# Softmax denominators of the two token halves in different rows: reciprocal over 256 columns, and the spread steps in new places

## The chip, the core and the metric

The kernel runs on one core of a Trainium2 chip. The core has a matrix engine (TensorE, PE in the profile; its weight loads are PEld), a vector engine (VectorE, DVE), an engine for activations (ScalarE, ACT), a general one (GpSimd, POOL) and SyncE (SP), which here only issues transfers. Each works through its own queue in order; they meet at semaphores. The metric is device microseconds (us) of one execution, as the median of several runs.

## The reference

The inputs are x (8 batches of 512 tokens of 512 values) and a context (8 batches of 120 tokens). Cut to what matters:

```python
Q = (layernorm(x) @ Wq.T + bq)   # 16 heads of 32
K, V = ctx @ Wk.T + bk, ctx @ Wv.T + bv
scores = einsum('bhqd,bhkd->bhqk', Q, K) / sqrt(32)
out = einsum('bhqk,bhkd->bhqd', softmax(scores), V)
expert = mean over 8 experts of (out @ We.T + be)
x = x + tanh(g_xattn) * (expert @ Wo.T + bo)
# then a gated feed-forward: logits = layernorm(x) @ w_gate, the best of 8 experts by
# argmax, at most 100 tokens per expert, layernorm(x) rows @ w_expert, scaled by the gate
x = x + tanh(g_ffn) * ffn(layernorm(x))
```

## The kernel before

A prologue of some 110 us transposes weights, builds keys and values of all batches and the product of the experts' mean with Wo (`mixT`). Then a loop runs over the 8 batches, software-pipelined: in the turn of batch 0 (step argument `b`) the queries of batch 1 are made, and so on. The order of the steps on each engine is a table written out by hand, of entries (step, how many batches ahead, part): `(spread_rden, 0, 2)` is part 2 of the spread for the current batch, `(q_tile, 1, 2)` the query tile 2 of the next batch. Each engine has its own table for the turns 0 to 6 (the loop), and another for the last turn (batch 7), where the rows that were chosen for an expert are gathered and multiplied too. Nothing but these tables and the semaphore waits in the steps sets the order. Nearly all products are written by one helper, so that they all have its line (L756); the names of their tiles tell them apart.

Steps that the change and the prediction speak of, with g or t for one of four parts:

- `scores` (ps<-q_stack,k_stack) makes the scores of four heads; `exp` on ACT writes them as `probs` (120 context tokens x 4 heads x 512 tokens, f32).
- `weight_sums` (ps<-probs,den_sel) sums probs over the context tokens, with one 120x32 matrix of a constant and zeros as weights. It adds up in `den_b` over the four g. The four matmuls (j = 0 to 3) write four different groups of 32 rows, and so run side by side. The profile has two records for each f32 matmul. Row 32j+m of `den_b` holds the sum of head 4g+j with g = m % 4: eight copies of each, over 512 tokens.
- `value_sums` (ps<-probs,v_all) makes the unnormalised attention, copied to `attn` by `value_out` (ACT).
- `reciprocal` (DVE) takes 1/x of the whole of `den_b`, 128x512. `rden_high` (ACT, f16) and `rden_low` (DVE) write from it `rden_both`, in which some copies hold the f16 value and others the rest.
- `spread_rden` (ps<-rden_both,head_sel) picks one head's two rows for each of the 128 output rows and writes them to a bank of 512 columns, once for each g. Parts 0 and 1 wait for `rden_low`; parts 2 and 3 for the `divide` that reads the bank before.
- `divide` (DVE, attn<-ps,attn) multiplies. `attn_high` (ACT) and `attn_low` (POOL, in the last turn DVE) cast the result to an f16 pair.
- `mix_high`, `mix_low` (ps<-mixT_..,attn_hi and ps<-mixT_hi,attn_lo) are the 8 and 4 products that make output tile t; part k of either waits for `attn_high` or `attn_low` of g = k. Each of the four tiles needs all four g.
- `q_tile` (12 products, ps<-xnT_..,wqT_..) is `q_begin` (6) and `q_end` (6). `q_high` (ACT) and `q_low` (DVE) read it out. `max_scores` (ps<-k_hi,q_hi, 16 small matmuls) makes rough scores, from which `maxima` (DVE, neg_max) takes a maximum; `max_scores` g waits for `maxima` g-1. `max_turn` (ps<-ident,neg_max) waits for the last one. After it `shift_row` (ACT) and a transfer write the row `shift` into `q_stack`, for which the next batch's `scores` waits. Ten more transfers (`q_stack<-q_hi`, `q_stack<-q_lo`) are issued by SP once `q_high` 3 and `q_low` 3 are done, ahead of that of `shift`.
- In the last turn `row_norm` (ACT, xb<-rows) normalises gathered rows, `row_turn` (ps<-ident,xb) turns them and `row_product` (ps<-wqT_..,xnT_..) multiplies them.

Of the kernel before, what the change touches and what calls it, by code (L numbers as in the profile page):

```python
# [79 lines left out]
def build(nc, x, ctx, g_xattn, g_ffn, Wq, bq, Wk, bk, Wv, bv, We, be, Wo, bo, w_gate, w_expert, b_expert, out):  # L80
# [7 lines left out]
    with ExitStack() as st:  # L88
        def sb(name, shape, dt):
            return st.enter_context(nc.sbuf_tensor(name, shape, dt))  # L90
# [663 lines left out]
        def _(e):  # L754
            def mm(out_, a, b, start=True, stop=True, **kw):
                return e.matmul(out_, a, b, start=start, stop=stop, **kw)  # L756
# [236 lines left out]
            def late_unit(i):  # L993
# [12 lines left out]

                (q_tile, 1, 1), (q_tile, 1, 2), (max_scores, 1, 1),
                (spread_rden, 0, 0), (spread_rden, 0, 1), (q_begin, 1, 3), (spread_rden, 0, 2), (spread_rden, 0, 3),
                (q_end, 1, 3),

                (mix_high, 0, 0), (mix_low_begin, 0, 0), (max_scores, 1, 2), (mix_low_end, 0, 0), (mix_high, 0, 1),
                (max_scores, 1, 3), (route_attn, 0, 0), (mix_low, 0, 1), (mix_begin, 0, 2), (max_turn, 1, 0),
# [35 lines left out]
            def last_product(_, t):  # L1048
# [10 lines left out]
                (value_sums, 0, 3),  # L1059
                (row_turn, 0, 0), (spread_rden, 0, 0), (spread_rden, 0, 1), (row_turn, 0, 1), (row_product, 0, 0),  # L1060
                (spread_rden, 0, 2), (spread_rden, 0, 3), (row_turn, 0, 2), (row_product, 0, 1), (row_turn, 0, 3),
                (mix_high, 0, 0), (mix_low, 0, 0), (mix_high, 0, 1), (mix_low, 0, 1), (route_attn, 0, 0),
# [8 lines left out]
        def _(e):  # L1071
# [137 lines left out]
            def x2_high(b, t):  # L1209
# [23 lines left out]
                (exp, 0, 1), (value_out, 0, 0), (gate_exp, -1, 0), (exp, 0, 2), (value_out, 0, 1),  # L1233
                (exp, 0, 3), (value_out, 0, 2), (value_out, 0, 3),
                (rden_high, 0, 0), (row_norm, 0, 0), (row_high, 0, 0), (row_norm, 0, 1), (attn_high, 0, 0),
                (attn_high, 0, 1), (row_high, 0, 1), (row_norm, 0, 2), (attn_high, 0, 2), (attn_high, 0, 3),
# [7 lines left out]
        def _(e):  # L1244
            e.memset(wgc[:, :, :], 0.0).then_inc(s_setv, 1)
            e.memset(den_sel[:, :, :], 0.0).then_inc(s_setv, 1)
            e.wait_ge(s_setv, 2)
            for g in range(NK):
                e.memset(den_sel[:, g, g::NK], 1.0 / (ATTN_SCALE * RDEN_SCALE)).then_inc(s_setv, 1)
            e.wait_ge(s_set, 2)  # L1250
            for g in range(NK):
                e.tensor_tensor(head_sel[:, g, :].rearrange("p (j d) -> p j d", d=DK),
                                ident[:, g::DK].unsqueeze(2).to_broadcast([P, HJ, DK]),
                                ident[:, NK + g::DK].unsqueeze(2).to_broadcast([P, HJ, DK]),
                                ALU.add).then_inc(s_setv, 1)
# [6 lines left out]
            e.wait_ge(s_setv, 13)  # L1262
            for half, unit_of in enumerate((1.0 / GATE_SCALE, 1.0 / (ATTN_SCALE * MIX_SCALE))):
# [227 lines left out]
            def add_table(b, _):  # L1491
# [97 lines left out]
            def last_out(b, t):  # L1589
# [192 lines left out]
```

## Time and profile before

| what | value |
|---|---|
| median of 3 runs | 443.79 us (441.75 to 445.31) |
| the profiled execution | 441.84 us, of it 440.1 us span |
| mean granted TensorE clock | 0.992 of full speed |
| PE busy | 420.4 us (96%) |
| DVE busy | 342.0 us (78%) |
| ACT busy | 223.3 us (51%) |
| POOL busy | 162.0 us (37%) |

The span is from the first to the last instruction of the program; the execution's own time is 1.74 us more. The durations below are those of the profiled execution. Busy time of PE counts each matmul from its start to the modelled end of its result, about 0.17 us after the next one may start, so the pace of the engine is read from one start to the next. In the loop the same step starts 38.1 us apart from one turn to the next (`max_scores` 3 at 208.22, 246.35, 284.49 us). In the last turn the first product of the mix starts at 398.27 us, and from there PE works to its last product without a gap between two starts that is longer than the work.

### The profile page before, as it was taken

The page shows a single profiled execution, that of the slowest core. Times are in us where ns is not written, and L with a number is a line of the kernel's source. Part 1 is how long each engine was busy: PE and PEld are TensorE (multiplying, and loading weights), DVE is VectorE, ACT ScalarE, POOL GpSimd, SP SyncE. Part 2 cuts the span into 40 slices and gives each one's busy share as a digit, 9 for nine tenths or more (in the row PEclk, how much of TensorE's full clock was granted, in tenths as well). Part 3 has the DMA queues.
Part 4 walks back from the last instruction along what each step waited for, and adds up shares of the span by engine and source line. Part 5 has one row for each costly group of instructions (what it writes and reads, how often), then busy time and mean ns, then how long its engine had stood idle before and what let it go on. Part 6 is the DMA issues. An engine that isn't in the chain of part 4 may idle for free.

```text
span 440.1 us, 8128 instructions
## 1 busy us (share of the span) xinstructions
PE 420.4 (96%) x2839; PEld 192.0 (44%) x2839; DVE 342.0 (78%) x675; ACT 223.3 (51%) x279; POOL 162.0 (37%) x149
## 2 busy tenths in 40 slices
PE   5899999899999999999999999999999998879996
PEld 4567464342344334434534443453444344334442
DVE  6438345785697999889889988988994698759983
ACT  4335313566572945666384475637537383556200
POOL 1005899315062319307132630703351082260460
PEclk9999999999999999999999999999999999969999
DMA  8998991356019605923860682295078044042573
GB/s 234 329 387 308 300 392 41 72 102 174 1 37 184 224 2 124 223 97 67 158 220 0 140 215 89 58 206 180 1 153 193 1 97 142 9 142 44 102 179 114
DMA packets 64843, 63.15 MB, mean 143 GB/s; under 512 B 41218, under 2 KB 44430, under 8 KB 64804
## 3 DMA queue, kind: packets, MB, share of 16 engines
q1 hardware_dynamic: 59691, 56.19, 48.0%
q0 software_dynamic: 1632, 3.49, 2.8%
q10 hardware_dynamic: 3480, 2.96, 2.1%
q8 instruction: 24, 0.39, 0.4%
q14 instruction: 16, 0.12, 0.1%
HBM read 29.59 MB, written 12.98 MB: 97 GB/s over the span
## 4 chain that ended last, share of the span: by engine, by line
PE 84%; ACT 5%; DVE 4%; DMA 3%; issue 2%; SPq 1%; ACTq 0%; POOLq 0%; DVEq 0%
PE ps L756 65%; PE ps L416 9%; DVE neg_max L1396 4%; ACT probs L1073 4%; PE ps L514 3%; PE ps L378 2%; DMA ctx_raw<-in_ctx_dram 1%; PE ps L961 1%; DMA rows<-out_dram,row_ix 1%; PE ps L537 1%; PE ps L488 1%; DMA q_stack<-shift 1%; PE ps L1019 1%; SPq L645 1%; ACT xb L1073 0%
## 5 line engine op out<-in xcount | busy, mean ns | idle before, releaser
L1073 ACT ACTIVATE probs<-ps 120x2048 f32<-120x2048 f32 x32 | 60.1, 1878 | 42.8 <-PE ps L756 42.8
L1705 POOL TENSOR_TENSOR attn_lo<-attn,attn_hi 128x512 f16<-128x512 f32 x28 | 31.5, 1158 | 112.6 <-ACT attn_hi L1073 112.6
L1396 DVE TENSOR_REDUCE neg_max<-ps 128x16 f32<-128x1920 f32 x32 | 68.6, 2142 | 1.0
L756 PE MATMUL ps<-xnT_hi,wqT_hi 128*128 128x512 f16 x128 | 48.6, 380 | 0.1
L756 PE MATMUL ps<-mixT_hi,attn_hi 128*128 128x512 f16 x128 | 48.5, 379 | 0.0
L756 PE MATMUL ps<-mixT_lo,attn_hi 128*128 128x512 f16 x128 | 48.5, 379 | 0.0
L756 PE MATMUL ps<-xnT_lo,wqT_hi 128*128 128x512 f16 x128 | 48.5, 379 | 0.0
L1650 POOL TENSOR_SCALAR veps<-mv 128x4 f32<-128x4 f32 (+1 forms) x17 | 4.6, 268 | 117.1 <-DVE mv L1283 81.4
L1713 POOL TENSOR_TENSOR xb<-xb,mix_bias 128x512 f32<-128x512 f32 x32 | 39.5, 1267 | 17.3 <-DVE cb_col L1339 17.3
L1073 ACT ACTIVATE q_hi<-ps,bias_cols 128x512 f16<-128x512 f32 x32 | 21.9, 686 | 36.0 <-PE ps L756 35.9
L756 PE MATMUL ps<-q_stack,k_stack 97*120 97x512 f16 x128 | 33.9, 387 | 2.2 <-DMA q_stack<-shift 0.8
L756 PE MATMUL ps<-mixT_hi,attn_lo 128*128 128x512 f16 x128 | 34.1, 380 | 0.3
L756 PE MATMUL ps<-probs,den_sel 120*32 120x512 f32 x256 | 34.1, 605 | 0.1
L756 PE MATMUL ps<-probs,v_all 120*32 120x512 f32 x256 | 33.3, 592 | 0.7 <-ACT attn L1073 0.7
L756 PE MATMUL ps<-xnT_hi,wqT_lo 128*128 128x512 f16 x128 | 32.8, 379 | 0.0
L1390 DVE SCALAR_TENSOR_TENSOR q_lo<-ps,bias_cols,q_hi 128x512 f16<-128x512 f32 x32 | 23.9, 746 | 11.4 <-ACT q_hi L1073 11.4
L1346 DVE RECIPROCAL rden<-ps 128x512 f32<-128x512 f32 x8 | 26.9, 3358 | 7.4 <-PE ps L756 7.4
L1073 ACT ACTIVATE q_stack<-q_hi 32x2048 f16<-32x2048 f16 x16 | 30.5, 1907 | 0.5
L1362 DVE SCALAR_TENSOR_TENSOR xb<-ps,xb 128x512 f32<-128x512 f32 x32 | 22.0, 686 | 8.6 <-PE ps L756 8.6
L1073 ACT ACTIVATE attn<-ps 128x512 f32<-128x512 f32 x32 | 19.0, 595 | 18.3 <-PE ps L756 18.2
L1073 ACT ACTIVATE attn_hi<-attn 128x512 f16<-128x512 f32 x32 | 19.7, 630 | 13.0 <-DVE attn L1356 13.0
L756 PEld LDWEIGHTS ps<-q_stack,k_stack 97*120 97x120 f16 x128 | 14.9, 132 | 20.0 <-ACT probs L1073 10.9
(246 smaller groups left out, 808.3 us busy)
## 6 DMA issues: line engine op xcount, KB each, us to landing
xb<-in_x_dram SPq DMA_DIRECT2D x8, 1024.0 KB, 6.0
q_stack<-q_hi SPq DMA_DIRECT2D x48, 128.0 KB
out_dram<-xb SPq DMA_DIRECT2D x6, 1024.0 KB, 5.9
raw<-in_L_xattn_We_dram SPq DMA_DIRECT2D x5, 1024.0 KB, 11.7
q_stack<-q_lo SPq DMA_DIRECT2D x32, 128.0 KB
xb<-in_L_xattn_We_dram SPq DMA_DIRECT2D x3, 1024.0 KB, 9.4
k_stack<-k_scratch SPq DMA_DIRECT2D x8, 360.0 KB, 4.0
out_dram<-xb SPq DMA_DIRECT2D x8, 256.0 KB, 2.2
```

What stands on the lines that cost most here:

```text
L378: ins = e.transpose(b[0:rows, i * cols:(i + 1) * cols], src_of(i), ident[0:cols, 0:cols])
L416: ins = e.matmul(out_, a(pa, k), b(pb_, k), start=(i == 0), stop=(i == len(steps) - 1))
L514: ins = e.matmul(b[:, :], left(i, o), right[j][:, o, :], start=(n == 0), stop=(n == len(steps) - 1))
L756: return e.matmul(out_, a, b, start=start, stop=stop, **kw)
L1073: return e.activation(out_, in_, func, **kw)
L1346: e.reciprocal(rden[:, :], den_b).then_inc(s_rec, 1)
L1362: e.scalar_tensor_tensor(out=row, in0=pair_b[t % 2], scalar=1.0 / (ATTN_SCALE * MIX_SCALE), in1=row, op0=ALU.mult, op1=ALU.add).then_inc(s ...
L1390: e.scalar_tensor_tensor(out=q_lo[:, g, :], in0=pair_b[g % 2], scalar=bias_cols[:, g:g + 1], in1=q_hi[:, g, :], op0=ALU.add, op1=ALU.subtr ...
L1396: e.tensor_reduce(neg_max[:, :, :, g], quad[:, :, 0:NT * SK].rearrange("p j (t s) -> p t j s", t=NT), AX.X, ALU.max, negate=True).then_inc ...
L1650: e.tensor_scalar(tmp, mean_var, EPS, None, ALU.add).then_inc(s_ve, 1)
L1705: e.tensor_tensor(attn_lo[:, g, :], attn[:, g, :], attn_hi[:, g, :], ALU.subtract).then_inc(s_alo, 1)
L1713: ins = e.tensor_tensor(row, row, mix_bias[:, :], ALU.add)
```

## The change

The denominators of tokens 0 to 255 go to rows 32j+m with m < 16, those of tokens 256 to 511 to rows with m >= 16, both in columns 0 to 255 of `den_b`. For this `weight_sums` issues for each g eight matmuls of 256 columns (h = 0, then h = 1, each with another selection matrix) in place of four of 512. The reciprocal and the two casts of it go over 256 columns, and `spread_rden` writes its bank by two matmuls of 256 columns, with a `head_sel` for each half. The tables change too: in the loop, spread parts 0 and 1 now stand inside query tile 2 and ahead of `max_scores` 1, `max_scores` 2 stands ahead of `mix_high` 0 (not inside `mix_low` 0), `maxima` 1 on DVE stands ahead of `q_low` 2 and the divides 2 and 3, and `rden_high` on ACT ahead of `q_high` 1; in the last turn the spreads stand ahead of `row_turn` 0 and 1.

```diff
-        den_sel = sb("den_sel", [SK, NK, DK], F32)
-        head_sel = sb("head_sel", [P, NK, P], F16)
+        den_sel = sb("den_sel", [SK, 2 * NK * DK + 24], F32)
+        head_sel = sb("head_sel", [P, 2, NK, P], F16)
...
-                for j in range(HJ):
-                    row = slice(j * DK, (j + 1) * DK)
-                    ins = mm(den_b[row, :], den_sel[:, g, :], probs[:, g % 2, j, :], start=(g == 0), stop=(g == NK - 1))
+                for h in range(2):
+                    sel = den_sel[:, (h * NK + g) * DK:(h * NK + g + 1) * DK]
+                    for j in range(HJ):
+                        row = slice(j * DK, (j + 1) * DK)
+                        ins = mm(den_b[row, 0:SH], sel, probs[:, g % 2, j, h * SH:(h + 1) * SH],
+                                 start=(g == 0 and h == 0), stop=(g == NK - 1 and h == 1))
...
-                mm(bank, head_sel[:, g, :], rden_both[:, :]).then_inc(s_bc, 1)
+                mm(bank[:, 0:SH], head_sel[:, 0, g, :], rden_both[:, :])
+                mm(bank[:, SH:S], head_sel[:, 1, g, :], rden_both[:, :]).then_inc(s_bc, 1)
...
-                e.reciprocal(rden[:, :], den_b).then_inc(s_rec, 1)
+                e.reciprocal(rden[:, :], den_b[:, 0:SH]).then_inc(s_rec, 1)
...
-                (reciprocal, 0, 0), (maxima, 1, 0), (rden_low, 0, 0), (q_low, 1, 1),
-                (divide, 0, 0), (divide, 0, 1), (q_low, 1, 2), (divide, 0, 2), (divide, 0, 3), (maxima, 1, 1),
+                (divide, 0, 0), (divide, 0, 1), (maxima, 1, 1), (q_low, 1, 2), (divide, 0, 2), (divide, 0, 3),
```

On PE in the loop, before: query tile 2 (its last products are the first row), `max_scores` 1, spreads 0 and 1, the first half of query tile 3, spreads 2 and 3.

```order
L756 MATMUL ps<-xnT_hi,wqT_lo 128x512 x4
L756 MATMUL ps<-k_hi,q_hi 128x120 x16
L756 MATMUL ps<-rden_both,head_sel 128x512 x2
L756 MATMUL ps<-xnT_hi,wqT_hi 128x512
L756 MATMUL ps<-xnT_lo,wqT_hi 128x512
L756 MATMUL ps<-xnT_hi,wqT_hi 128x512
L756 MATMUL ps<-xnT_lo,wqT_hi 128x512
L756 MATMUL ps<-xnT_hi,wqT_hi 128x512
L756 MATMUL ps<-xnT_lo,wqT_hi 128x512
L756 MATMUL ps<-rden_both,head_sel 128x512 x2
```

The same place of PE with the change, from the spreads 0 and 1 on:

```order
L757 MATMUL ps<-rden_both,head_sel 128x256 x4
L757 MATMUL ps<-xnT_hi,wqT_hi 128x512
L757 MATMUL ps<-xnT_lo,wqT_hi 128x512
L757 MATMUL ps<-xnT_hi,wqT_lo 128x512 x4
L757 MATMUL ps<-k_hi,q_hi 128x120 x16
```

The spreads moved up past half a query tile, and `max_scores` 1 moved down behind them.

On DVE in the loop, before, from the reciprocal to `maxima` 2 (neg_max is `maxima`, attn is `divide`):

```order
L1346 RECIPROCAL rden<-ps 128x512
L1396 TENSOR_REDUCE neg_max<-ps 128x16
L1351 SCALAR_TENSOR_TENSOR rden_both<-rden,low_row,rden_hi 128x512
L1390 SCALAR_TENSOR_TENSOR q_lo<-ps,bias_cols,q_hi 128x512
L1356 TENSOR_TENSOR attn<-ps,attn 128x512 x2
L1390 SCALAR_TENSOR_TENSOR q_lo<-ps,bias_cols,q_hi 128x512
L1356 TENSOR_TENSOR attn<-ps,attn 128x512 x2
L1396 TENSOR_REDUCE neg_max<-ps 128x16
L1390 SCALAR_TENSOR_TENSOR q_lo<-ps,bias_cols,q_hi 128x512
L1396 TENSOR_REDUCE neg_max<-ps 128x16
```

And with the change:

```order
L1346 RECIPROCAL rden<-ps 128x256
L1396 TENSOR_REDUCE neg_max<-ps 128x16
L1351 SCALAR_TENSOR_TENSOR rden_both<-rden,low_row,rden_hi 128x256
L1390 SCALAR_TENSOR_TENSOR q_lo<-ps,bias_cols,q_hi 128x512
L1356 TENSOR_TENSOR attn<-ps,attn 128x512 x2
L1396 TENSOR_REDUCE neg_max<-ps 128x16
L1390 SCALAR_TENSOR_TENSOR q_lo<-ps,bias_cols,q_hi 128x512
L1356 TENSOR_TENSOR attn<-ps,attn 128x512 x2
L1390 SCALAR_TENSOR_TENSOR q_lo<-ps,bias_cols,q_hi 128x512
L1396 TENSOR_REDUCE neg_max<-ps 128x16
```

`maxima` 1 (the second neg_max) moved from behind the divides 2 and 3 to ahead of them.

On PE in the last turn, with the change, from the last `value_sums` to the first `row_product` (xb is `row_turn`); before, the order was row_turn 0, spreads 0 and 1, row_turn 1, row_product 0, spreads 2 and 3, row_turn 2:

```order
L757 MATMUL ps<-probs,v_all 32x512 x8
L757 MATMUL ps<-rden_both,head_sel 128x256 x4
L1016 MATMUL ps<-ident,xb 128x100 x4
L757 MATMUL ps<-rden_both,head_sel 128x256 x4
L1016 MATMUL ps<-ident,xb 128x100 x4
L757 MATMUL ps<-wqT_hi,xnT_hi 128x512
```

Both pairs of spreads now stand ahead of the first row product.

## Rows read from the trace of the kernel before

**Rows 1.** The page: busy time of PE and the others.

```profile
PE 420.4 (96%) x2839; PEld 192.0 (44%) x2839; DVE 342.0 (78%) x675; ACT 223.3 (51%) x279; POOL 162.0 (37%) x149
```

**Rows 2.** Timeline of PE in one turn: start, us, what, idle before and its releaser.

```profile
230.15 1.06 PE L756 MATMUL ps<-probs,den_sel 120*32 120x512 f32 x8
231.03 1.04 PE L756 MATMUL ps<-probs,v_all 120*32 120x512 f32 x8
232.01 0.39 PE L756 MATMUL ps<-xnT_hi,wqT_hi 128*128 128x512 f16 x1
...
237.29 0.39 PE L756 MATMUL ps<-k_hi,q_hi 32*128 32x120 f16 x16
237.61 0.61 PE L756 MATMUL ps<-rden_both,head_sel 128*128 128x512 f16 x2
...
243.60 0.39 PE L756 MATMUL ps<-k_hi,q_hi 32*128 32x120 f16 x16
244.04 0.39 PE L756 MATMUL ps<-mixT_hi,attn_lo 128*128 128x512 f16 x1
...
246.35 0.39 PE L756 MATMUL ps<-k_hi,q_hi 32*128 32x120 f16 x16 [0.20 <-DVE neg_max L1396]
```

**Rows 3.** Timeline of DVE in the same turn.

```profile
231.28 3.36 DVE L1346 RECIPROCAL rden<-ps 128x512 f32<-128x512 f32 x1 [0.86 <-PE ps L756]
...
239.91 1.28 DVE L1356 TENSOR_TENSOR attn<-ps,attn 128x512 f32<-128x512 f32 x2
241.10 2.15 DVE L1396 TENSOR_REDUCE neg_max<-ps 128x16 f32<-128x1920 f32 x1
243.17 0.74 DVE L1390 SCALAR_TENSOR_TENSOR q_lo<-ps,bias_cols,q_hi 128x512 f16<-128x512 f32 x1
244.05 2.16 DVE L1396 TENSOR_REDUCE neg_max<-ps 128x16 f32<-128x1920 f32 x1
```

**Rows 4.** Timelines of ACT, POOL and SP in the same turn.

```profile
240.62 1.23 ACT L1073 ACTIVATE attn_hi<-attn 128x512 f16<-128x512 f32 x2 [0.63 <-DVE attn L1356]
241.75 0.67 ACT L1073 ACTIVATE q_hi<-ps,bias_cols 128x512 f16<-128x512 f32 x1
...
239.47 4.51 POOL L1705 TENSOR_TENSOR attn_lo<-attn,attn_hi 128x512 f16<-128x512 f32 x4 [15.07 <-ACT attn_hi L1073]
...
246.25 3.49 SPq L645 DMA_DIRECT2D q_stack<-q_lo  x4
250.26 0.52 SPq L645 DMA_DIRECT2D q_stack<-shift  x1
```

**Rows 5.** Groups by line and form, whole span: count, busy us and mean ns of one, idle before.

```profile
L1451 DVE RECIPROCAL gate<-l_sum 128x4 f32<-128x4 f32 x8 | 1.4, 180 | 0.3
L756 PEld LDWEIGHTS ps<-probs,den_sel 120*32 120x32 f32 x256 | 5.0, 108 | 10.5 <-issue 9.6 <-ACT probs L1073 0.3
```

**Rows 6.** Timelines of ACT and PE in the last turn.

```profile
384.72 0.60 ACT L1073 ACTIVATE attn<-ps 128x512 f32<-128x512 f32 x1 [1.19 <-PE ps L756]
386.29 0.81 ACT L1073 ACTIVATE xb<-rows,row_shift,table 100x512 f32<-100x512 f32 x1
...
387.15 0.93 PE L1019 MATMUL ps<-ident,xb 100*128 100x100 f32 x4 [2.50 <-ACT xb L1073]
387.88 1.06 PE L756 MATMUL ps<-rden_both,head_sel 128*128 128x512 f16 x2
389.37 0.93 PE L1019 MATMUL ps<-ident,xb 100*128 100x100 f32 x4 [0.44 <-ACT xb L1073]
390.10 0.63 PE L756 MATMUL ps<-wqT_hi,xnT_hi 128*128 128x512 f16 x1
...
394.36 0.59 PE L756 MATMUL ps<-rden_both,head_sel 128*128 128x512 f16 x2
394.79 0.51 PE L1019 MATMUL ps<-ident,xb 100*128 100x100 f32 x4
```

**Rows 7.** One stretch of the last turn: busy time by engine, granted clock, DMA.

```profile
388.00:390.00 2.00, 1.56 (x7) 0.65 (x6) 1.35 (x3) 1.35 (x3) 1.46 (x2) 0.50 0.46 150
```

More of the change, by code:

```diff
@@ L59 @@
 HALF = B // 2
+SH = S // 2
 QK_SCALE = 16.0
@@ L1005, in _ @@
                 (places, -1, 0), (q_end, 1, 0), (values, 0, 2), (max_scores, 1, 0), (values, 0, 3),
[L1007 to L1011, printed above, removed]
+                (q_tile, 1, 1), (q_begin, 1, 2), (spread_rden, 0, 0), (spread_rden, 0, 1), (q_end, 1, 2),
+                (max_scores, 1, 1), (q_begin, 1, 3), (spread_rden, 0, 2), (spread_rden, 0, 3), (q_end, 1, 3),
+                (max_scores, 1, 2), (mix_high, 0, 0), (mix_low, 0, 0), (mix_high, 0, 1),
                 (max_scores, 1, 3), (route_attn, 0, 0), (mix_low, 0, 1), (mix_begin, 0, 2), (max_turn, 1, 0),
@@ L1059, in _ @@
                 (value_sums, 0, 3),
-                (row_turn, 0, 0), (spread_rden, 0, 0), (spread_rden, 0, 1), (row_turn, 0, 1), (row_product, 0, 0),
-                (spread_rden, 0, 2), (spread_rden, 0, 3), (row_turn, 0, 2), (row_product, 0, 1), (row_turn, 0, 3),
+                (spread_rden, 0, 0), (spread_rden, 0, 1), (row_turn, 0, 0), (spread_rden, 0, 2), (spread_rden, 0, 3),
+                (row_turn, 0, 1), (row_product, 0, 0), (row_turn, 0, 2), (row_product, 0, 1), (row_turn, 0, 3),
                 (mix_high, 0, 0), (mix_low, 0, 0), (mix_high, 0, 1), (mix_low, 0, 1), (route_attn, 0, 0),
@@ L1225, in _ @@
                 (value_out, 0, 2), (value_out, 0, 3), (gate_exp, -1, 0),
-                (q_high, 1, 1), (rden_high, 0, 0), (q_high, 1, 2), (attn_high, 0, 0), (attn_high, 0, 1),
+                (rden_high, 0, 0), (q_high, 1, 1), (attn_high, 0, 0), (q_high, 1, 2), (attn_high, 0, 1),
                 (attn_high, 0, 2), (attn_high, 0, 3), (q_high, 1, 3),
@@ L1233, in _ @@
                 (exp, 0, 1), (value_out, 0, 0), (gate_exp, -1, 0), (exp, 0, 2), (value_out, 0, 1),
-                (exp, 0, 3), (value_out, 0, 2), (value_out, 0, 3),
-                (rden_high, 0, 0), (row_norm, 0, 0), (row_high, 0, 0), (row_norm, 0, 1), (attn_high, 0, 0),
+                (exp, 0, 3), (value_out, 0, 2), (rden_high, 0, 0), (value_out, 0, 3),
+                (row_norm, 0, 0), (row_high, 0, 0), (row_norm, 0, 1), (attn_high, 0, 0),
                 (attn_high, 0, 1), (row_high, 0, 1), (row_norm, 0, 2), (attn_high, 0, 2), (attn_high, 0, 3),
@@ L1245, in _ @@
             e.memset(wgc[:, :, :], 0.0).then_inc(s_setv, 1)
-            e.memset(den_sel[:, :, :], 0.0).then_inc(s_setv, 1)
+            e.memset(den_sel[:, :], 0.0).then_inc(s_setv, 1)
             e.wait_ge(s_setv, 2)
-            for g in range(NK):
-                e.memset(den_sel[:, g, g::NK], 1.0 / (ATTN_SCALE * RDEN_SCALE)).then_inc(s_setv, 1)
+            for h in range(2):
+                first = h * (NK * DK + DK // 2)
+                e.memset(den_sel[:, first:first + NK * (DK + 1)].rearrange("p (g c) -> p g c", g=NK)[:, :, 0:DK // 2:NK],
+                         1.0 / (ATTN_SCALE * RDEN_SCALE)).then_inc(s_setv, 1)
             e.wait_ge(s_set, 2)
[L1251 to L1254, printed above, removed]
+            for h in range(2):
+                row_of = ident[:, :].rearrange("p (j h c g) -> p h c g j", h=2, c=NK, g=NK)
+                e.tensor_tensor(head_sel[:, h, :, :].rearrange("p g (j d) -> p g j d", d=DK),
+                                row_of[:, h, 0, :, :].unsqueeze(3).to_broadcast([P, NK, HJ, DK]),
+                                row_of[:, h, 1, :, :].unsqueeze(3).to_broadcast([P, NK, HJ, DK]),
                                 ALU.add).then_inc(s_setv, 1)
@@ L1600, in _ @@
                 (read_places, -1, 0), (enter_places, -1, 0), (expert_low, 0, 1), (add_table, -1, 0), (row_index, 0, 0),
-                (reciprocal, 0, 0), (rden_low, 0, 0), (row_lo, 0, 0), (divide, 0, 0), (divide, 0, 1), (row_lo, 0, 1),
-                (last_attn_low, 0, 0), (last_attn_low, 0, 1), (divide, 0, 2), (divide, 0, 3), (last_attn_low, 0, 2),
+                (reciprocal, 0, 0), (rden_low, 0, 0), (divide, 0, 0), (divide, 0, 1), (row_lo, 0, 0), (divide, 0, 2),
+                (divide, 0, 3), (row_lo, 0, 1), (last_attn_low, 0, 0), (last_attn_low, 0, 1), (last_attn_low, 0, 2),
                 (last_attn_low, 0, 3), (row_lo, 0, 2), (row_bias, 0, 0), (row_out, 0, 0), (row_lo, 0, 3),
```

19 lines of the change are left out of this document (7 added, 12 removed).

## Prediction

> **What bounds the kernel now.** I read the page first: PE is busy for 96% of the span, so only work of PE and waits of PE count, and another engine counts through them [rows 1]. Next comes the timeline of PE in one turn of the loop, of which seven follow each other at a period of 38.1 us, alike to some hundredths [rows 2]. The reader is to see how small the holes are. Between 230 and 250 us PE waits four times: about 0.07 us for `q_low` 1 behind the spreads 0 and 1, 0.12 us for the last `attn_low` at 244.04, about 0.27 us for `maxima` 2 at 246.35, and 0.05 us for `maxima` 3, some 0.5 us in all. I take each as the time from one start to the next less that of the same step elsewhere; only the third shows in brackets, since a result takes longer than the pace. Then I read who ends these waits, on DVE, ACT and POOL [rows 3, 4]. Last comes the final turn, where PE has its one long hole: no record starts between the last `value_sums` and 387.15, and behind it the granted clock is 0.50, the lower of the two levels (1.2 against 2.4 GHz) [rows 6, 7]. From 398.3 us PE runs without a hole to its last product, so what is won or lost ahead of that counts in full.
>
> **Work of PE.** In `weight_sums` four f32 matmuls of 512 columns become eight of 256. The columns are the same, and the four groups of 32 rows still run side by side. The four of 512 take 0.88 us from start to start (230.15 to 231.03) [rows 2]; each of their two rounds costs some hundredths beyond the array's own time. Two rounds more per g would cost from 0.004 us (what the second round shows) to 0.03 us (the first). I take the lower, since in the middle of a run the next weights are in place: 32 x 0.004 = 0.13 us in all. The spreads become 4 x 0.108 us instead of 2 x 0.216 (two took 0.43, from 394.36 to 394.79 [rows 6]); 0.1 us in all for twice as many matmuls. The changes of shape of PE's tile stay as many.
>
> A rule speaks against the halving. The four matmuls have the same 120 rows of the array and differ in its columns, and their weights show 108 ns each [rows 5]; yet two rounds of them and their loads pass in 0.88 us, so the loads lie under the matmuls. The Trainium skill, "TensorE: Matmul & The Clock Gate", section "Part 3: Packing small matmuls — row/col tiling", says that a weight load overlaps matmuls in flight only where its row group differs, and by it each new round would lay its load open. By that rule the sum would grow by the second rival's price below; the trace of before disagrees with it.
>
> **DVE, ACT and the spreads.** The reciprocal of 4 columns takes 0.18 us, that of 512 takes 3.36 us [rows 3, 5], so one column costs (3.36 - 0.18) / 508 = 6.3 ns and 256 take 1.76 us: 1.60 us less. It starts at 231.28 as before, ends at 233.0, `maxima` 0 is done at 235.2 (2.15 us) and `rden_low`, with half of its columns, at about 235.6. PE comes to the spreads 0 and 1 after three halves of query tiles: tile 1 starts at 232.01, and two tiles take up to 237.29, so 18 of 24 products end at 235.9 [rows 2]. No wait: the shorter reciprocal pays for the earlier place. With 3.36 us the same spreads would have waited about 1.5 us. `rden_high` ahead of `q_high` 1 waits until 233.0, while query tile 1 ends at 234.8, so it holds nobody up. The wait for `q_low` 1 goes: -0.07 us.
>
> **The chain that now ends last.** `max_scores` 1 starts at 237.29 + 0.43 = 237.72, behind the spreads. The rest is a walk through the new order with the old durations:
> - DVE: `maxima` 1 starts 0.45 us after its `max_scores` (243.60 to 244.05), at 238.17; DVE had nothing to do for 0.5 us before. It holds DVE for 2.07 us (241.10 to 243.17), `q_low` 2 for 0.66 (0.74 less the 0.08 by which such instructions overlap), and the divides 2 and 3 run from 240.90 to 242.18. Before, these ended at 239.91 + 1.28 = 241.19 [rows 3]. The 1.6 us won go into `maxima` 1, and the divides come 1.0 us later.
> - ACT and POOL: `attn_high` 3 ended at 241.85, and now ends at 242.84. POOL ran its four `attn_low` without a pause, 1.13 us each, from 239.47 to 243.98 [rows 4]. Now the first two run early, POOL pauses, and part 2 starts only when `attn_high` 2 is there, at 242.31. Part 3 ends at 242.31 + 4.51 / 2 = 244.6, which is 0.6 us later.
> - PE: behind `max_scores` 1 (0.32) come half of tile 3, two spreads and the other half (2.59 + 0.43), and `max_scores` 2 at 241.16, ended at 241.48. The eight products of `mix_high` 0 end at 243.34, with 0.14 us of waiting for `attn_high` 3. After three products of `mix_low` 0, at 243.99, PE waits for `attn_low` 3 until 244.65. Before, the same product started at 244.04 [rows 2]. That is 0.61 us late.
> - Given back: `mix_high` 1 then ends late enough that `maxima` 2 (244.1 to 246.3) is done before `max_scores` 3 wants it, so the wait of 0.27 us goes. `max_scores` 3 starts at 246.69 and not at 246.35: **0.34 us late**. `maxima` 3, `max_turn` and all that follows stay late by as much.
>
> The transfers to `q_stack` move too. They start when `q_high` 3 ends, before at 242.42 (241.75 + 0.67), now at about 243.4, since `q_high` 3 stands behind `attn_high` 3. The ten of them keep SP busy until 249.74 + 1.0 = 250.75, where `shift` went out at 250.26 and would now be ready at 250.60 [rows 4]. So the transfer of `shift` goes from waiting for ACT to waiting for the queue, 0.5 us late, and `scores` finds it just in time, with its 0.2 us of slack used up. I count nothing and keep 0.3 us a turn for the range.
>
> Loop: 7 x 0.34 = 2.4 us, and 0.2 us for the matmuls, **+2.6 us**.
>
> **The last turn.** The spreads 0 and 1 can start when `value_out` 3 ends at 385.3 (384.72 + 0.60) instead of at 387.88. But `row_turn` 0 waits for ACT's `row_norm` (386.29 to 387.11), which waits for a gathered row, and `row_turn` 1 for the next one; neither knows of the denominators [rows 6]. So the first row product stays at 390.10 if the clock stays as it was, and only the spreads 2 and 3 leave the path behind it (394.36 to 394.79): **-0.43 us**. The clock is the open point. While it is low, `row_turn` 0 and 1 take 0.73 us each, 0.37 more than at full clock, and the 12 products 4.26 us (390.10 to 394.36) against 2.59: together 2.4 us. If it stays high, the first turn ends 0.37 us earlier, ACT's next step follows, the products start at about 389.35, and the mix starts at 395.3: -3.0 us in place of -0.43. The hole from 384.6 to 387.15 now has 0.43 us of spreads in it, and the one from 387.5 to 389 has 0.43 more. That is little; I hold the fall of the clock for somewhat likelier than not.
>
> **Sum.** 441.84 + 2.6 - 0.4 = 444.0 us for an execution like the profiled one. The median of the runs before lies 1.95 us above that execution, and I carry the difference over: 443.79 + 2.15 = **445.9 us**.
>
> **Rivals.**
> - The clock stays high in the last turn. For it: PE has two more bits of work in the hole. Against it: the hole stays mostly empty, since the gathered rows set it. 443.79 + 2.6 - 3.0 = 443.4 us. Chance 0.27.
> - Slower: the weight loads of the added rounds lie open. Place: the 32 groups of `weight_sums`, two more rounds in each. Price: up to 108 ns a round, 64 x 0.108 = 6.9 us, so 452.8 us; from 35 ns a round on it is over 1% slower than before. Against it: the 0.88 us of the rows. This is the result of the page's rule above. Chance 0.06.
> - Slower: `q_stack` becomes the end of the chain. With `shift` landing or the ten transfers 0.3 to 0.6 us later than I have it, PE waits at each `scores` 0: 2 to 4 us more, 448 to 450 us. Chance 0.12.
> - Faster: POOL's last cast is in time after all, because the divides or `maxima` 1 run earlier than in my walk. Then the 0.3 us of waits go and none comes: 7 x -0.3 - 0.4 to -3.0, so 441.3 to 438.7 us. The walk would have to be wrong by 0.6 us. Chance 0.09.
> - The change doesn't do what it says, the time of the reciprocal not going by columns: 7 x 1.5 us, 456 us. The 0.18 us of the small one excludes it nearly: 0.01.
> - The forecast itself, 444.5 to 447.5 us: 0.45.
>
> **How the numbers follow.** No change that a measurement of this kernel can tell is one within 1%, 4.4 us. The forecast, the high clock, most of the faster case and a third of the `q_stack` case lie inside. Faster by over 1% has 0.06, slower 0.15, no change 0.79. The range goes from 441.0 (into the faster case, below the high clock with a shorter wait) to 449.5 us, most of the `q_stack` case; what is left out is the open weight loads and the ends, under 0.2.
>
> **What would show it.** A reciprocal of 1.7 to 1.8 us; eight den_sel matmuls in 0.88 to 0.91 us; no wait at the spreads 0 and 1. A pause of POOL between the second and third `attn_low`, and a wait of PE of 0.5 to 0.8 us for the last one in each turn; none for `maxima` 2. A period of 38.5 us instead of 38.1. In the last turn a spread right behind `value_out` 3, and either a stretch of 6 to 7 us at 0.50 or none. I am wrong if the period is shorter than 38.1, or if PE waits for `q_stack` in the loop.

## The result, and the profile after

| what | before | after |
|---|---|---|
| median of 20 runs of each, on the same chips | 442.88 us (441.22 to 445.31) | 445.18 us (443.50 to 448.99) |
| ratio, 95% interval | | 1.0059 (1.0042 to 1.0076) |
| profiled execution | 441.84 us, span 440.1 | 445.22 us, span 443.5 |
| period of the loop (max_scores 3 to the next) | 38.13 us | 38.5 us; one turn 38.92 |

The kernel became slower by 2.3 us by the medians, by 2.6 us (1.9 to 3.4) by the ratio: 0.6%. That is under the 1% which the prediction took as the least that can be told, but with 20 runs of each the interval of the ratio excludes 1. The forecast was 445.9 us, +2.15. The first line of the page after, against [rows 1]: DVE lost 13.0 us of work (342.0 to 329.0, eight reciprocals at 1.6 us each) and the span grew.

```profile
PE 422.4 (95%) x3127; PEld 204.6 (46%) x3127; DVE 329.0 (74%) x671; ACT 221.4 (50%) x279; POOL 163.3 (37%) x149
```

Groups by line and form after, over the whole span (count, busy us and mean ns of one, idle before), against [rows 5]:

```profile
L1346 DVE RECIPROCAL rden<-ps 128x256 f32<-128x256 f32 x8 | 14.1, 1757 | 7.5 <-PE ps L757 7.5
L757 PEld LDWEIGHTS ps<-probs,den_sel 120*32 120x32 f32 x512 | 13.4, 109 | 16.0 <-issue 9.6 <-ACT probs L1070 0.3
```

The reciprocal is at 1.757 us and the loads have doubled in number. Next PE after, in the turn of [rows 2] (start, us, what, idle before and its releaser). The whole turn starts 1.80 us later here: 231.95 answers to 230.15.

```profile
231.95 1.07 PE L757 MATMUL ps<-probs,den_sel 120*32 120x256 f32 x16
232.84 1.04 PE L757 MATMUL ps<-probs,v_all 120*32 120x512 f32 x8
...
237.49 0.38 PE L757 MATMUL ps<-xnT_lo,wqT_hi 128*128 128x512 f16 x1
237.70 0.60 PE L757 MATMUL ps<-rden_both,head_sel 128*128 128x256 f16 x4
...
245.15 0.81 PE L757 MATMUL ps<-mixT_hi,attn_lo 128*128 128x512 f16 x3
246.45 0.39 PE L757 MATMUL ps<-mixT_hi,attn_lo 128*128 128x512 f16 x1 [0.49 <-POOL attn_lo L1705]
...
248.50 0.39 PE L757 MATMUL ps<-k_hi,q_hi 32*128 32x120 f16 x16
```

Three things stand here. Sixteen records of `weight_sums` go from 231.95 to 232.84, 0.89 us where eight took 0.88. The spreads follow a product of the query tile at the usual 0.21 us: no wait. And the product behind `mix_low` 0's first three comes 1.30 us after their start, where three take 0.65: PE waits 0.65 us for POOL. `max_scores` 3 (248.50) has lost its bracket for neg_max.

DVE after in the same turn, against [rows 3], from the reciprocal through `maxima` 1 and the second pair of divides:

```profile
233.09 1.76 DVE L1346 RECIPROCAL rden<-ps 128x256 f32<-128x256 f32 x1 [0.88 <-PE ps L757]
...
239.97 2.16 DVE L1396 TENSOR_REDUCE neg_max<-ps 128x16 f32<-128x1920 f32 x1 [0.56 <-PE ps L757]
...
242.71 1.28 DVE L1356 TENSOR_TENSOR attn<-ps,attn 128x512 f32<-128x512 f32 x2
```

ACT and POOL after, against [rows 4]:

```profile
243.42 1.23 ACT L1070 ACTIVATE attn_hi<-attn 128x512 f16<-128x512 f32 x2 [2.57 <-DVE attn L1356]
```

```profile
239.55 1.16 POOL L1705 TENSOR_TENSOR attn_lo<-attn,attn_hi 128x512 f16<-128x512 f32 x1 [13.36 <-ACT attn_hi L1070]
240.92 1.15 POOL L1705 TENSOR_TENSOR attn_lo<-attn,attn_hi 128x512 f16<-128x512 f32 x1 [0.21 <-ACT attn_hi L1070]
244.12 2.27 POOL L1705 TENSOR_TENSOR attn_lo<-attn,attn_hi 128x512 f16<-128x512 f32 x2 [2.05 <-ACT attn_hi L1070]
```

Read from below: POOL pauses 2.05 us for `attn_high` 2; ACT waited 2.57 us for the divides; DVE made the divides behind `maxima` 1; and `maxima` 1 waited 0.56 us for its `max_scores`, which PE issues behind the spreads now. The reciprocal gave up 1.60 us ahead of the divides, and 2.07 us of `maxima` 1 took its place.

Then what the forecast counted at nothing. SP and PE after, at the hand-over of queries to `scores` two turns earlier (an SPq line is the time that SP took to issue a transfer, not the time to its landing):

```profile
171.64 3.81 SPq L646 DMA_DIRECT2D q_stack<-q_lo  x4
175.50 0.59 SPq L646 DMA_DIRECT2D q_stack<-shift  x1
```

```profile
178.04 1.04 PE L757 MATMUL ps<-q_stack,k_stack 97*120 97x512 f16 x4 [0.24 <-issue]
...
372.12 1.04 PE L757 MATMUL ps<-q_stack,k_stack 97*120 97x512 f16 x4 [1.36 <-DMA q_stack<-shift]
```

The four `q_lo` transfers are issued from 171.64 to 175.45 without a pause for ACT, `shift` right behind them, where in [rows 4] 0.5 us lie between the two: in this turn the queue, and not ACT, sets when `shift` goes. So it went out late and PE lost 0.42 us (38.92 for 38.5). The bracket says issue, but the product could only start once the row had landed, which the trace puts at 177.70. In the turn of [rows 4] it is not so:

```profile
249.04 2.50 SPq L646 DMA_DIRECT2D q_stack<-q_lo  x4
252.41 0.52 SPq L646 DMA_DIRECT2D q_stack<-shift  x1
```

Here the queue is free at 251.54, `shift` waits for ACT as before, and PE loses nothing. What differs is how long SP takes to issue the ten transfers: 6.24 us here (245.30 to 251.54), 7.57 us two turns earlier.

The last row above is the last turn: its `scores` are 3.83 us behind those of before (372.12 to 368.29), `max_scores` 3 ahead of it 3.30 us (364.05 to 360.75), so 0.53 us more were lost. This is another thing. `shift` goes out 0.06 us after ACT has written it, but takes longer to land, as the chain that ended last shows, before and then after:

```profile
364.66 3.27 DMA q_stack<-shift
```

```profile
367.99 3.78 DMA q_stack<-shift
```

From issue to landing the last `shift` takes 2.9 to 3.8 us in the profiles of the twelve kernels, 3.68 in e4 and 3.54 in e9, which don't have the late queue; in the turns of the loop it is 2.1 to 2.2 us almost everywhere. So these 0.5 us can't be put down to the change.

Last the final turn, PE against [rows 6]:

```profile
389.31 0.60 PE L757 MATMUL ps<-rden_both,head_sel 128*128 128x256 f16 x4 [0.81 <-ACT attn L1070]
391.12 0.93 PE L1016 MATMUL ps<-ident,xb 100*128 100x100 f32 x4 [1.21 <-ACT xb L1070]
391.84 1.06 PE L757 MATMUL ps<-rden_both,head_sel 128*128 128x256 f16 x4
393.34 0.93 PE L1016 MATMUL ps<-ident,xb 100*128 100x100 f32 x4 [0.44 <-ACT xb L1070]
394.06 0.63 PE L757 MATMUL ps<-wqT_hi,xnT_hi 128*128 128x512 f16 x1
...
398.57 0.51 PE L1016 MATMUL ps<-ident,xb 100*128 100x100 f32 x4
```

And a stretch of it, with the granted clock as the number behind POOL's, against [rows 7]:

```profile
392.00:394.00 2.00, 1.56 (x9) 0.96 (x7) 1.38 (x3) 1.92 (x4) 1.70 (x2) 0.50 0.60 154
```

The spreads are where the table puts them, the clock is at its lower level again (0.50), and the row products of turn 0 lead straight into row_turn 2: from the first product on 4.51 us pass (394.06 to 398.57), before 4.69 (390.10 to 394.79). The way from the first row product to the first mix product is 7.79 us against 8.17, so 0.38 us shorter.

**Account of the profiled execution,** by how far the same step is behind that of before: the first `max_scores` 3 0.14 us (86.49 to 86.35), the eighth 3.30 (364.05 to 360.75), so 3.16 in seven periods, 0.42 of them the unlucky turn; `scores` of the last turn 3.83; the first row product 3.96; the first mix product 3.58; the end of the span 3.36. What took the last 0.22 us off I did not find. That execution is the worse for its long turn and for the late landing ahead of the last `scores`; the medians say 2.3.

### The profile page after: what moved, and what is told of

It is laid out like the page before. It is cut to its first block, busy times and chain, and to the rows that moved or that the text cites. A ratio compares the mean times of both kernels' runs of the same rounds, so it can differ in the third digit from the quotient of the medians.

```text
span 443.5 us, 8700 instructions
## 1 busy us (share of the span) xinstructions
PE 422.4 (95%) x3127; PEld 204.6 (46%) x3127; DVE 329.0 (74%) x671; ACT 221.4 (50%) x279; POOL 163.3 (37%) x149
## 4 chain that ended last, share of the span: by engine, by line
PE 33%; issue 24%; POOL 10%; DVE 4%; DMA 2%; SPq 2%; ACT 1%; POOLq 0%; DVEq 0%; ACTq 0%
PE ps L757 31%; POOL attn_lo L1705 5%; POOL rstd L1652 3%; DVE bn_raw L1278 2%; SPq L646 2%; POOL std L1661 1%; DMA q_stack<-shift 1%; ACT probs L1070 1%; DMA rows<-out_dram,row_ix 1%; PE ps L959 1%; PE ps L1016 1%; POOL veps L1650 1%; DVE neg_max L1396 0%; ACT xb L1070 0%; DVE mv L1283 0%
## 5 line engine op out<-in xcount | busy, mean ns | idle before, releaser
L757 PE MATMUL ps<-probs,den_sel 120*32 120x256 f32 x512 | 34.3, 385 | 0.1
L757 PEld LDWEIGHTS ps<-mixT_hi,attn_lo 128*128 128x128 f16 x128 | 11.9, 97 | 22.3 <-POOL attn_lo L1705 6.9
```

## The experiments

Each ran beside the kernel before on its own chip: medians of before were 442.40 us for the first four, 442.17 for e5 to e8, 442.32 for the last two. Ratios are to that; the ratio of the change is 1.0059.

**e1: the halves with the old loop.** All edits of the change but the loop's order, which is that of before. Edit to the kernel after (DVE; PE's and ACT's tables likewise):

```diff
-                (divide, 0, 0), (divide, 0, 1), (maxima, 1, 1), (q_low, 1, 2), (divide, 0, 2), (divide, 0, 3),
+                (divide, 0, 0), (divide, 0, 1), (q_low, 1, 2), (divide, 0, 2), (divide, 0, 3), (maxima, 1, 1),
```

> The change with the loop's three tables (PE, DVE, ACT) put back as they were; halved denominators, 256-column reciprocal and the new last turn stay. My theory, that the loss is the new order (maxima 1 ahead of the divides, so that attn_low 3 comes late): no wait of 0.66 us for attn_low 3, period of a turn 38.05 to 38.15 us instead of 38.5, time 442.3 us (0.2 to 0.8 under before). Rival, that the doubled matmuls of the denominators and spreads cost it: the period stays at 38.4 to 38.5, time 445 us.

Measured: 442.25 us, ratio 0.9986 (0.9971 to 1.0001), period 38.10. So neither the 256 columns nor the doubled `weight_sums` cost anything that shows; the loss of the change lies in the loop's order. With the old order the shorter reciprocal buys next to nothing either: 0.03 us a turn, and some tenths of a microsecond in all, in which the new last turn has its part.

**e2: the new order with the full reciprocal.** The kernel before with all tables of the change.

> The kernel before with all tables of the change but whole denominators: reciprocal over 512 columns, spreads of 512. Theory: the earlier place of the spreads is paid for by the shorter reciprocal, so here PE waits some 1.5 us ahead of the spreads 0 and 1 in each turn, all behind it is late, period 40.0 us (39.6 to 40.3), time 456 us (453 to 458). Rival, that the reciprocal has slack there and the halving buys nothing: period 38.5, time 445 us.

Measured: 456.05 us, ratio 1.0313 (1.0284 to 1.0342), period 40.0 in the plain turns. PE and DVE of e2, each one row of the timeline:

```profile
244.28 0.59 PE L756 MATMUL ps<-rden_both,head_sel 128*128 128x512 f16 x2 [1.34 <-issue]
```

```profile
238.16 3.36 DVE L1345 RECIPROCAL rden<-ps 128x512 f32<-128x512 f32 x1 [0.86 <-PE ps L756]
...
243.45 0.73 DVE L1350 SCALAR_TENSOR_TENSOR rden_both<-rden,low_row,rden_hi 128x512 f16<-128x512 f32 x1
```

`rden_low` ends at 244.18 and the spreads start 0.10 us later, 1.71 us after the product ahead of them (242.57), which is 1.50 over the pace. The wait of 1.5 us that the prediction gave the early spreads with a full reciprocal is there, once a turn. The halves are what makes the order possible: worth 11 us with it, next to nothing without it (e1).

**e3: `maxima` 1 back behind the divides.** The spreads stay early:

```diff
-                (divide, 0, 0), (divide, 0, 1), (maxima, 1, 1), (q_low, 1, 2), (divide, 0, 2), (divide, 0, 3),
+                (divide, 0, 0), (divide, 0, 1), (q_low, 1, 2), (divide, 0, 2), (divide, 0, 3), (maxima, 1, 1),
```

On PE `max_scores` 2 moves to where before had it, ahead of the last product of `mix_low` 0.

> The change with maxima 1 put back behind the divides 2 and 3 on DVE, and max_scores 2 back inside mix_low 0 on PE; the early spreads and the halves stay. Theory: attn_low 3 is in time, the wait of 0.66 us goes, one of about 0.25 us for maxima 2 comes back; period 38.05 us (37.95 to 38.15), time 442.2 us. Rival, that the early spreads themselves (max_scores 1 pushed 0.43 us later) are the loss: the period stays above 38.35, time 444.5 us or more.

Measured: 441.09 us, ratio 0.9975 (0.9964 to 0.9987), 1.1 us under what was expected; period 38.10. PE and POOL of e3 (its lines count 7 more):

```profile
243.24 0.39 PE L757 MATMUL ps<-k_hi,q_hi 32*128 32x120 f16 x16
243.56 0.39 PE L757 MATMUL ps<-mixT_hi,attn_lo 128*128 128x512 f16 x1
...
245.99 0.39 PE L757 MATMUL ps<-k_hi,q_hi 32*128 32x120 f16 x16 [0.31 <-DVE neg_max L1403]
```

```profile
240.89 2.27 POOL L1712 TENSOR_TENSOR attn_lo<-attn,attn_hi 128x512 f16<-128x512 f32 x2 [0.93 <-ACT attn_hi L1077]
```

POOL's pause is 0.93 us and not 2.05, its last cast ends at 243.16, and the product at 243.56 finds it done. Instead the wait for `maxima` 2 is back (0.31). One entry of DVE's table, together with PE's for `max_scores` 2, is the whole loss of the loop's order, and two waits exchange as the walk said. The two entries moved together; no run separates them, and that it is DVE's which counts is read from POOL's pause.

**e4: all spreads early, no maximum between the divides.** From e3 it was a step to drop both waits. Edit to the kernel after:

```diff
-                (max_scores, 1, 1), (q_begin, 1, 3), (spread_rden, 0, 2), (spread_rden, 0, 3), (q_end, 1, 3),
+                (spread_rden, 0, 2), (spread_rden, 0, 3), (max_scores, 1, 1), (q_tile, 1, 3),
...
-                (max_scores, 1, 2), (mix_high, 0, 0), (mix_low, 0, 0), (mix_high, 0, 1),
+                (mix_high, 0, 0), (max_scores, 1, 2), (mix_low, 0, 0), (mix_high, 0, 1),
...
-                (divide, 0, 0), (divide, 0, 1), (maxima, 1, 1), (q_low, 1, 2), (divide, 0, 2), (divide, 0, 3),
+                (divide, 0, 0), (divide, 0, 1), (divide, 0, 2), (divide, 0, 3), (q_low, 1, 2), (maxima, 1, 1),
```

> The change with the spreads 2 and 3 moved too, to right behind query tile 2, max_scores 1 behind them, the four divides in a row on DVE ahead of q_low 2 and maxima 1, and max_scores 2 between mix_high 0 and mix_low 0. Theory: divides 2 and 3 end 2.8 us sooner, POOL runs its four casts nearly without a pause and none is waited for, maxima 2 and 3 come in time; nearly all waits of the turn go, period 37.65 us (37.6 to 37.75), q_stack's transfers start 1.4 us sooner than in the change; time 439.5 us (438.8 to 440.5). Rival, that another wait takes their place (q_stack or the second maxima): period 38.0 or more, time 442 us or more.

Measured: 438.77 us, at the lower end of what was expected; ratio 0.9915 (0.9895 to 0.9936), period 37.72. PE and POOL of e4:

```profile
241.46 0.39 PE L757 MATMUL ps<-k_hi,q_hi 32*128 32x120 f16 x16
241.78 1.04 PE L757 MATMUL ps<-mixT_hi,attn_lo 128*128 128x512 f16 x4
...
244.48 0.39 PE L757 MATMUL ps<-k_hi,q_hi 32*128 32x120 f16 x16
```

```profile
236.30 1.16 POOL L1705 TENSOR_TENSOR attn_lo<-attn,attn_hi 128x512 f16<-128x512 f32 x1 [13.38 <-ACT attn_hi L1070]
237.67 3.38 POOL L1705 TENSOR_TENSOR attn_lo<-attn,attn_hi 128x512 f16<-128x512 f32 x3 [0.21 <-ACT attn_hi L1070]
```

POOL's last cast ends at 241.05, ahead of the 241.78 at which `mix_low` 0 begins, and PE has no wait left in this stretch. Here the 1.6 us of the reciprocal reach PE, as 0.4 us a turn, and there was hardly more to win, since PE's holes summed to 0.5.

**e5: the old last turn.** The kernel after with the last turn's tables of before on PE, ACT and DVE, so `row_turn` 0 ahead of the spreads:

```diff
-                (spread_rden, 0, 0), (spread_rden, 0, 1), (row_turn, 0, 0), (spread_rden, 0, 2), (spread_rden, 0, 3),
-                (row_turn, 0, 1), (row_product, 0, 0), (row_turn, 0, 2), (row_product, 0, 1), (row_turn, 0, 3),
+                (row_turn, 0, 0), (spread_rden, 0, 0), (spread_rden, 0, 1), (row_turn, 0, 1), (row_product, 0, 0),
+                (spread_rden, 0, 2), (spread_rden, 0, 3), (row_turn, 0, 2), (row_product, 0, 1), (row_turn, 0, 3),
```

> The change with the last turn's tables put back (PE, ACT, DVE); the loop is the changed one. Theory: the row path there hangs on gathered rows, so the new order of the last turn is worth only the 0.43 us of the spreads 2 and 3, less if something else hides it: 445.6 us, 0.2 to 0.5 above the change, and the clock falls to 0.50 in the last turn in both. Rival, that the early spreads keep PE busy enough to matter: 2 us or more above the change in time.

Measured: 445.99 us, ratio 1.0094 (1.0073 to 1.0114). By the ratios that is 1.5 us above the change, where 0.2 to 0.5 was expected, and I can't place the rest. The run says less than hoped: its profiled execution has two long turns (38.61 and 39.11, together 0.72 us) where that of the change has one, and the clock fell later. From the last `value_sums` to the first mix product it takes 14.11 us (388.20 to 402.31) against 14.42 in the change (387.43 to 401.85), so in these two profiles the old last turn isn't the slower one. The -0.43 us of the prediction are neither shown nor refuted by it; the next pair of runs prices them better.

**e6 and e10: keeping the clock up.** To price the low clock, products that nobody reads are added in the holes of the last turn (work beyond the reference's). Edit to the kernel after, 6 ahead of `row_turn` 0 and 5 ahead of `row_turn` 1:

```diff
+            def filler(_, n):
+                e.wait_ge(s_ex, 4 * B)
+                for _ in range(n):
+                    mm(quad[:, 3, :], mixT_hi[:, 0, 0:P], mixT_hi[:, 1, :])
...
-                (spread_rden, 0, 0), (spread_rden, 0, 1), (row_turn, 0, 0), (spread_rden, 0, 2), (spread_rden, 0, 3),
-                (row_turn, 0, 1), (row_product, 0, 0), (row_turn, 0, 2), (row_product, 0, 1), (row_turn, 0, 3),
+                (spread_rden, 0, 0), (spread_rden, 0, 1), (filler, 0, 6), (row_turn, 0, 0), (spread_rden, 0, 2),
+                (spread_rden, 0, 3), (filler, 0, 5), (row_turn, 0, 1), (row_product, 0, 0), (row_turn, 0, 2), (row_product, 0, 1), (row_turn, 0, 3),
```

> The change with 6 and 5 products of 512 columns on constants into a free bank added on PE in the last turn, ahead of row_turn 0 and of row_turn 1, where PE has nothing to do (added work that no result uses). Theory: with them the granted clock does not fall there; row_turn 0 and 1 take 0.35 us and the first row product 2.6 us; the mix of the last turn starts 2.0 to 2.6 us sooner; 442.9 us. Rival, that the low clock costs nothing beyond the waits for rows, or falls all the same: within 0.5 us of the change, or above it by the added products' time (11 x 0.22 = 2.4 us).

Measured: 443.57 us, 0.7 above what was expected; ratio 1.0025 (1.0009 to 1.0042). PE and the stretch of e6:

```profile
391.24 1.46 PE L757 MATMUL ps<-mixT_hi 128*128 128x512 f16 x6
...
394.88 0.38 PE L757 MATMUL ps<-wqT_hi,xnT_hi 128*128 128x512 f16 x1
...
397.47 0.51 PE L1016 MATMUL ps<-ident,xb 100*128 100x100 f32 x4
```

```profile
392.00:394.00 2.00, 2.00 (x15) 1.18 (x13) 0.76 (x2) 1.35 (x3) 1.65 (x2) 1.00 0.59 154
```

The clock stays at 1.00, and the row products take 2.59 us (394.88 to 397.47) instead of 4.51. The kernel before with 8 and 3 such products:

> The kernel before with 8 and 3 filler products of 512 columns on constants (no result uses them) in the last turn, ahead of row_turn 0 and of row_turn 1. Theory, that the fall of the clock there is a loss of its own, in both kernels, and no matter of the denominators: the clock stays high, 2 us gained, 440.3 us (439.6 to 441.3). Rival, that the gain seen with the changed last turn needs its early spreads: no gain, 442.3 us.

Measured: 440.37 us, ratio 0.9952 (0.9936 to 0.9969). The low clock costs about 2 us in either kernel: 1.5 us from the ratios after, 2.1 us before. PE of e10:

```profile
391.43 0.38 PE L756 MATMUL ps<-wqT_hi,xnT_hi 128*128 128x512 f16 x1
...
394.02 0.59 PE L756 MATMUL ps<-rden_both,head_sel 128*128 128x512 f16 x2
394.46 0.51 PE L1019 MATMUL ps<-ident,xb 100*128 100x100 f32 x4
```

With the clock at 1.00 in both, this pair prices the place of the spreads 2 and 3: from the first row product to `row_turn` 2 it is 3.03 us in e10, which has them between (391.43 to 394.46), and 2.59 in e6, which doesn't. That is the 0.43 us of the prediction.

**e7: e4 and e6 together.** The edits are those of the two.

> All spreads early in the loop (as in the fourth experiment) and the filler products of the last turn together. Theory: two separate gains that add up, 5.7 us and 2.3 us under the change: 437.2 us (436.3 to 438.5). Rival, that they overlap: 439.5 us.

Measured: 435.69 us, ratio 0.9858 (0.9836 to 0.9879), 6.5 us under before and 0.6 under the range that was expected. The gains add: by the ratios e4 lies 3.8 us under before, and e7 2.5 us further down.

**e8: quarters.** `weight_sums` in matmuls of 128 columns, so that each g has four more rounds of weights. Edit to the kernel after:

```diff
-                    for j in range(HJ):
-                        row = slice(j * DK, (j + 1) * DK)
-                        ins = mm(den_b[row, 0:SH], sel, probs[:, g % 2, j, h * SH:(h + 1) * SH],
+                    for c in range(0, SH, P):
+                        for j in range(HJ):
+                            row = slice(j * DK, (j + 1) * DK)
+                            ins = mm(den_b[row, c:c + P], sel, probs[:, g % 2, j, h * SH + c:h * SH + c + P],
...
```

> The change with each denominator matmul of 256 columns split into two of 128 with the same weights, loaded anew: eight rounds for each g in place of four. Theory, that loads are hidden and a round costs a few ns: each group grows from 0.887 to about 0.90 us (up to 0.95), time 445.3 to 447 us. Rival by the rule that a load lies open unless its row group differs: 4 x 32 x 0.108 = 13.8 us more, 459 us.

Measured: 446.52 us, ratio 1.0093 (1.0076 to 1.0111), with one turn of 39.18. PE of e8:

```profile
232.76 1.08 PE L757 MATMUL ps<-probs,den_sel 120*32 120x128 f32 x32
233.66 1.04 PE L757 MATMUL ps<-probs,v_all 120*32 120x512 f32 x8
```

A group takes 0.90 us with 32 records, 0.89 with 16, 0.88 with 8. Four rounds more cost 0.01 us, not four loads of 109 ns. The rule of the Trainium skill that the prediction weighed ("TensorE: Matmul & The Clock Gate", "Part 3: Packing small matmuls — row/col tiling") would, taken as strictly as it stands there, put e8 about 14 us above the change; the measurement decides against it for tiles that differ in columns. The median of e8 is 1.3 us above that of the change (1.5 by the ratios). Its groups account for 32 x 0.010 = 0.3 us of that; its long turn may be a part of the rest, which no run settles.

**e9: `q_high` 3 ahead of `attn_high` 3.** Does PE's wait for `shift` in the long turns come from the order on ACT? Edit to the kernel after:

```diff
-                (attn_high, 0, 2), (attn_high, 0, 3), (q_high, 1, 3),
+                (attn_high, 0, 2), (q_high, 1, 3), (attn_high, 0, 3),
```

> The change with q_high 3 ahead of attn_high 3 on ACT in the loop, not behind it. Theory, that the turns of 38.9 us in the change are waits of scores 0 for q_stack, whose transfers start only when q_high 3 is done: they start 0.5 to 0.6 us sooner, no turn takes 38.9 us any more, the wait ahead of the last turn's scores shrinks by up to 0.5 us; the period stays at 38.5 us, since attn_low 3 still ends last (attn_high 3 comes just before POOL is free for it). Time 444.6 us, 0.3 to 1.0 under the change. Rival, that the long turns come from the traffic itself whenever it starts: turns of 38.9 us stay, time as the change.

Measured: 444.10 us, ratio 1.0050 (1.0033 to 1.0067); its periods from the second on are 38.27, then 38.49 or 38.50 five times, none long. The link shows in the time from the end of `q_high` 3 to the first `scores` when nothing is waited for, which is what the ten transfers and `shift` have: 10.48 us before (242.42 to 252.90), 10.4 to 10.6 in e1, e3, e4 and e9, 9.83 in the change (245.22 to 255.05), 9.8 in e2, e5 and e8, which share its order. That time is the room for the queue. The ten transfers take 6.2 to 7.9 us to issue, differently from turn to turn of one kernel, whatever its order; why, no run shows. With the order of the change PE waits where they take more than about 7.2 us (7.57 us: 0.42 us lost; 7.26 in e5: 0.10; 7.76 in e5: 0.61). With 0.65 us more room the same estimate gives 7.8 us, and the longest issue there is 7.74 us (e10). Periods 0.1 to 0.7 us above their neighbours stand in the profiles of the change, e2, e5, e6 and e8, one or two each, and in none of before, e1, e3, e4, e7, e9 and e10. (The 40.29 us of e2 is a `shift` that landed late, not a late queue.) The ratio alone, 0.1% under that of the change, wouldn't show it, and each kernel has one profile.

## Why the prediction was right

- **Work of PE.** 0.88 to 0.91 us for the group was named, 0.89 found; e8 shows that the cost of a round is 2 to 3 thousandths of a microsecond. The rival of open weight loads is out.
- **The spreads.** No wait, as said; e2 shows the 1.5 us that would have been there.
- **The walk.** Less the 1.80 us by which the turn starts later: `maxima` 1 starts at 238.17 (said 238.17), the divides end at 242.19 (242.18), `attn_high` 3 at 242.85 (242.84), the last `attn_low` at 244.59 (244.6), `max_scores` 3 starts at 246.70 (246.69). Old durations in a new order sufficed to a hundredth, as no duration on this path but the reciprocal's changed. e3 confirms the cause by undoing it.
- **The sum of the loop.** 0.34 + 0.03 us a turn was said; from the fourth turn on the plain ones show 0.36, 0.37, 0.42 and 0.37.
- **The last turn.** -0.43 said; with the clock up e6 and e10 show 0.44. That the profile of the change shows -0.38 between the first row product and the first mix product is partly luck: with the same tables this way takes 7.43 us in e1, 7.54 in e3, 7.89 in e4 and 8.53 in e8, by where the low clock falls. The clock fell again, as was held for somewhat likelier than not.
- **`q_stack`: the term mis-sized.** "I count nothing" was wrong in part, and the working behind it too. For the turn of [rows 4] it had the ten transfers keep SP busy for 7.24 us, as before, so that `shift` would wait for the queue in each turn. In that turn they took 6.24 us, the queue was free 0.84 us before `shift` was written, and `shift` went out when ACT was done: at 252.41, which less the 1.80 us is 250.61, the very 250.60 at which the prediction has it ready. What is true of it: `q_high` 3 ends later, the room for the queue shrank from 10.48 to 9.83 us, as e9 shows, and the queue then decides in the turns in which it is slow. In the profiled execution that cost 0.42 us in one turn and 0.05 in another, not the 2 to 4 us of the rival. That "PE waits for `q_stack` in the loop" stood among what would make me wrong; it did, in one turn.
- **The total.** The level, 445.9 us, is 0.7 us too high, since it was taken from the median of three runs before, 443.79, which over twenty is 442.88. The difference is the number that was argued: +2.15 said, +2.3 measured by the medians, 1.9 to 3.4 by the ratio. The terms of the loop and of the last turn are confirmed one by one; that the sum comes this close is partly luck, since the waits for `q_stack`, counted at nothing, lie in the measured number.

## What to carry to other kernels

A shorter instruction on an engine that isn't the bound is worth only what the waits of the bounding engine are; write down these holes first (0.5 us a turn here), since they are the most that can be won. What fills the place that it leaves matters more than the saving: a 2 us reduction let in ahead of two divides, at the head of a chain ACT, POOL, PE, cost 0.4 us a turn against the same kernel without that step (e3), while an order that lets nothing in between won 0.4 (e4). And where durations don't change, a walk through the new order with the old durations gives each start to a hundredth. The issuing of transfers, whose time differs by over 1 us from turn to turn, is the exception: room that a new order takes from it is paid for in the turns in which it is slow.

## What was not expected of the hardware

The clock falls at different moments, and for different times, in last turns that are nearly alike. Stretches of one microsecond of the last turn after, with the granted clock third from the end:

```profile
390.00:391.00 1.00, 0.00 (x0) 0.00 (x0) 1.00 (x2) 0.75 (x1) 0.70 (x2) 1.00 0.49 168
391.00:392.00 1.00, 0.88 (x5) 0.86 (x6) 0.01 (x1) 0.06 (x1) 0.69 (x2) 0.55 0.49 131
...
397.00:398.00 1.00, 1.00 (x4) 0.40 (x3) 0.82 (x2) 0.00 (x0) 0.56 (x1) 0.54 0.39 156
```

It fell behind a microsecond with no record of PE (PE's last records start at 389.3 to 389.6) and came back 6.8 us later, in the middle of the row products. Before, it fell within 386 to 387, also in a stretch with no record of PE, for 6.8 us too. In e9, whose last turn is that of the change, it fell only in 393 to 394, at the start of the row products, and was back 3.4 us later. Work in the hole doesn't explain this. In e5 the hole was as empty as before (its `row_turn` 0 at 391.97 with 2.71 us of idle ahead of it), and yet the clock was up through the hole and fell in 393 to 394, again for 3.4 us:

```profile
392.00:393.00 1.00, 0.97 (x8) 0.66 (x8) 0.00 (x0) 0.43 (x2) 0.69 (x2) 1.00 0.41 140
393.00:394.00 1.00, 0.18 (x1) 0.18 (x2) 0.90 (x2) 0.77 (x2) 0.76 (x1) 0.83 0.50 111
```

What sets the moment these runs leave open. A later fall spares the row turns (the first two are 1.85 us apart in e9, 2.22 in the change) and still hits the row products. In the profiles of e6, e7 and e10, with eleven products of 0.22 us that nobody reads in the holes, it didn't fall there; that is worth 1.5 to 2.1 us by the medians and ratios of e6 and e10.
